# Block attention's own queries moved from ScalarE to GpSimd, with the counts and step masks re-ordered behind them

## The reference

```python
q, k = rope(x @ Wq.T), rope(x @ Wk.T)              # 16 heads of 16, 256 positions, 8 blocks of 32
km   = k.reshape(B, 8, 32, H, d).mean(axis=2)      # mean key of a block
gate = einsum('bshd,bnhd->bhsn', q, km)            # future blocks -1e30, own block +1e30
sel  = blocks among the 4 largest gates            # per query and head
scores = where(sel & causal, q @ k.T * d ** -0.5, -1e30)
o = softmax(scores) @ v                            # then normalised per head, times Wo
```

## Time and profile before

| | before |
|---|---|
| median of 3 runs | 682.59 us (682.48 to 682.76) |
| the profiled execution, its own time | 682.5 us |
| its span, first to last instruction | 680.3 us |
| TensorE busy | 655.0 us (96%) |
| VectorE busy | 493.7 us (73%) |
| ScalarE busy | 418.0 us (61%) |
| GpSimd busy | 298.1 us (44%) |
| mean granted TensorE clock | 0.999 |

### The profile page before, as it was taken

The page is one execution under the profiler, slowest core; times in us unless marked ns, Lnnn a source line. Parts: engine busy times, 40 slices in busy tenths (PEclk is TensorE's granted clock), DMA queues, the critical chain, the costliest instruction groups (busy, mean ns, idle before and its releaser), DMA issues.

```text
span 680.3 us, 13835 instructions
## 1 busy us (share of the span) xinstructions
PE 655.0 (96%) x4756; PEld 573.6 (84%) x4756; DVE 493.7 (73%) x1434; ACT 418.0 (61%) x1084; POOL 298.1 (44%) x301
## 2 busy tenths in 40 slices
PE   5999999999999999999999989999989999999997
PEld 3777888898888998888888865556889999999996
DVE  7897867877878687887797798897565544645444
ACT  3856158788888888798854689997553222222221
POOL 1584155556464655452344328997543500400000
PEclk9999999999999999999999999999999999999999
DMA  8902034444525344342740000303000000000000
GB/s 319 373 2 101 1 121 135 153 149 134 192 91 184 119 165 128 107 151 93 279 178 1 1 1 2 110 1 125 2 1 1 1 16 2 1 16 1 2 16 16
DMA packets 26725, 59.43 MB, mean 87 GB/s; under 512 B 3146, under 2 KB 12748, under 8 KB 26272
## 3 DMA queue, kind: packets, MB, share of 16 engines
q1 hardware_dynamic: 23584, 50.35, 21.7%
q0 software_dynamic: 3072, 8.20, 3.6%
HBM read 48.24 MB, written 10.49 MB: 86 GB/s over the span
## 4 chain that ended last, share of the span: by engine, by line
PE 75%; DVE 10%; ACT 7%; POOL 3%; issue 3%; DMA 0%; SPq 0%; ACTq 0%; POOLq 0%; DVEq 0%
PE bank L2284 11%; PE bank L2049 7%; PE bank L1983 6%; PE bank L2333 5%; PE bank L2040 5%; PE bank L2307 5%; PE bank L2145 4%; PE bank L2069 4%; PE bank L2060 4%; PE bank L1990 4%; ACT sb L1211 3%; PE bank L2111 3%; PE bank L2192 3%; PE bank L2347 2%; PE bank L1923 2%
## 5 line engine op out<-in xcount | busy, mean ns | idle before, releaser
L1072 ACT ACTIVATE sb<-bank,sb 128x256 f32<-128x256 f32 x128 | 59.5, 471 | 38.8 <-DVE sb L1573 37.8
L1279 ACT ACTIVATE h_parts<-sb 128x256 fp32r<-128x256 f32 x56 | 23.4, 418 | 72.6 <-DVE sb L1831 43.8
L2049 PE MATMUL bank<-sb 128*128 128x256 f32 x256 | 66.1, 381 | 0.0
L1822 DVE TENSOR_TENSOR sb<-sb,bank 128x256 f32<-128x256 f32 x56 | 23.4, 419 | 58.1 <-ACT sb L1235 58.1
L1573 DVE TENSOR_REDUCE sb<-bank 128x2 f32<-128x512 f32 x64 | 43.7, 683 | 27.1 <-PE bank L2049 26.6
L2284 PE MATMUL bank<-rounded,b_hi 128*128 128x256 f32 x224 | 63.1, 282 | 0.0
L2284 PE MATMUL bank<-rounded,b_lo 128*128 128x256 f32 x224 | 62.9, 281 | 0.0
L2284 PE MATMUL bank<-am_lo,b_hi 128*128 128x256 f32 x224 | 62.9, 281 | 0.0
L839 POOL DMA_INDIRECT expert_out<-sb x32 | 33.0, 1031 | 61.3 <-DVE sb L1515 47.4
L1235 ACT ACTIVATE sb<-bank 128x256 f32<-128x256 f32 x56 | 21.4, 382 | 61.6 <-PE bank L2284 61.6
L1079 ACT ACTIVATE sb<-sb 128x256 f32<-128x256 f32 x128 | 57.8, 505 | 0.1
(11 more groups left out here) (321 smaller groups left out, 1941.5 us busy)
## 6 DMA issues: line engine op xcount, KB each, us to landing
sb<-in_w_gate_up SPq DMA_DIRECT2D x32, 368.0 KB, 2.9
sb<-in_w_down SPq DMA_DIRECT2D x32, 256.0 KB, 2.7
sb<-in_w_pair SPq DMA_DIRECT2D x8, 704.0 KB, 4.0
expert_out<-sb SPq DMA_DIRECT2D x1, 4096.0 KB, 22.8
sb<-expert_out SPq DMA_DIRECT2D x8, 512.0 KB, 6.8
sb<-in_w SPq DMA_DIRECT2D x1, 1792.0 KB, 12.2
sb<-in_b SPq DMA_DIRECT2D x1, 1792.0 KB, 8.1
sb<-in_sw_up SPq DMA_DIRECT2D x1, 1536.0 KB, 9.0
```

The lines of the kernel that those rows point to most:

```text
L1072: act.activation(probs[:, u % 4, q, :], bank[3 + u % 2][:, q * S:(q + 1) * S], ACT.Exp, scale=-1.0, bias=row_min[:, u % 4, q:q + 1], accum ...
L2049: mm = pe.matmul(bank[3 + u % 2][:, q * S:(q + 1) * S], qb[i][:, h, b * S + q * P:b * S + (q + 1) * P], keys[:, h, b * S:(b + 1) * S], sta ...
```

## The change

Four edits, with what they need to be legal:

1. The own queries of groups 2 to 7 are no longer made by ScalarE inside the quads. GpSimd makes them before its counts, one `tensor_tensor` of 128x512 per group for both parities, into a new place `q_later`. That place is in `rounded`, where `x1T_hi` and `a13_hi` lie until the eighth low fill, so GpSimd waits for `fill_mm` 8; later the high parts of the masked activations go there, so those wait for the scores (`bl_s`).
2. GpSimd counts batch 1 alone and batches 2 and 3 together. The biases and the load of `b13` wait accordingly.
3. The product with the step mask and its split come behind the split of `b13`, the first activations and the first network weights.
4. `kmean` is written by two `tensor_tensor` instead of 16 `tensor_scalar`, and `own_bias(0)` comes behind the thirteenth fill copy instead of the sixteenth.

```diff
@@ block attention's buffers
-        q_par = r2.take(2, 2, S)
+        q_par = [r2.take(2, S) for _ in range(2)]
...
+            q_later = over("q_later", SB_COLS + 3 * TOK, 3 * TOK)
+        q_par += [Strip(q_later, at * TOK + G * 2 * S, 2 * S).take(2, S) for at in (1, 0, 2) for G in range(2)]
@@ count
-            ranks = rank.rearrange("p t (h n) -> p (t h) n", n=NB)[:, at:at + QT * H1, :]
+            ranks = rank.rearrange("p t (h n) -> p (t h) n", n=NB)[:, at:at + heads.stop - heads.start, :]
@@ sync
-            sp.wait_ge(rest_count, COUNTS * (B - 1))
+            sp.wait_ge(rest_count, COUNTS * 2)
             sp.dma_start(b13, t["b13"]).then_inc(ab_in, 16)
@@ gpsimd
+            pool.wait_ge(qkT_out, NT)
+            pool.wait_ge(bl_q, 4)
+            pool.wait_ge(fill_mm, 8)
+            for G in range(2, GROUPS):
+                b, k = G // 2, G % 2
+                pool.tensor_tensor(q_par[G], along(qkT[:, k, b * S:(b + 1) * S], (1, 2)), along(table("par_scale"), (2, S)),
+                                   ALU.mult).then_inc(bl_q, 2)
+
             pool.wait_ge(kmean_set, 5)
             pool.wait_ge(rest_beats, NB - 1)
-            for b in range(1, B):
-                count(pool, QT * H1 * b, slice(QT * H1 * (b - 1), QT * H1 * b), beats_rest, rest_beats, rest_count, COUNTS * (b - 1))
+            for n, (first, last) in enumerate(((1, 2), (2, B))):
+                count(pool, QT * H1 * first, slice(QT * H1 * (first - 1), QT * H1 * (last - 1)), beats_rest, rest_beats, rest_count,
+                      COUNTS * n)
...
-            pool.wait_ge(step_mask, 1)
-            for j in range(2):
-                pool.wait_ge(low_rank, j + 1)
-                pool.tensor_tensor(am_step[j], am_step[j], step_maskT, ALU.mult).then_inc(low_rank, 1)
-
             pool.wait_ge(ab_in, 32)
...
-            pool.wait_ge(low_rank, 4)
...
                 for k in kinds:
+                    if c < 2 and c + k:
+                        pool.wait_ge(bl_s, HG * {(0, 1): 4, (1, 0): 6, (1, 1): 8}[c, k])
...
-            low_rank_parts(0)
+            pool.wait_ge(low_rank, 2)
+            low_rank_parts(0, (0,))
             pool.wait_ge(w3_in, 32)
             for n, kind in enumerate(("x1", "w13")):
...
+            pool.wait_ge(step_mask, 1)
+            for j in range(2):
+                pool.tensor_tensor(am_step[j], am_step[j], step_maskT, ALU.mult).then_inc(low_rank, 1)
+            pool.wait_ge(low_rank, 4)
+            low_rank_parts(0, (1,))
             low_rank_parts(1, (0,))
@@ scalar
             def own_queries(G, par):
-                at_least(act, bl_s, HG * (G - 1))
-                act.activation(q_par[:, G % 2, par, :], qkT[:, k, b * S:(b + 1) * S], ACT.Copy,
+                act.activation(q_par[G][:, par, :], qkT[:, k, b * S:(b + 1) * S], ACT.Copy,
...
             def own_bias(G):
-                    act.wait_ge(rest_count, COUNTS * b)
+                    act.wait_ge(rest_count, COUNTS * min(b, 2))
...
+                if n == len(fills()) - 4:
+                    own_bias(0)
...
-            own_bias(0)
             own_bias(1)
             for Q in range(QUADS + 1):
...
-                if 1 < Q < QUADS and Q // 2 + 1 < GROUPS:
-                    own_queries(Q // 2 + 1, Q % 2)
@@ vector
-                for h in range(HG):
-                    at = (k * HG + h) * NB
-                    dve.tensor_scalar(kmean[:, k, :, at:at + NB], kblock[:, k, :].rearrange("p (b n) -> p b n", n=NB),
-                                      table("head_mean")[:, h:h + 1], None, ALU.mult).then_inc(kmean_done, 1)
+                own = slice(k * HG * NB, (k + 1) * HG * NB)
+                dve.tensor_tensor(kmean[:, k, :, own].rearrange("p b (h n) -> p b h n", n=NB),
+                                  along(kblock[:, k, :].rearrange("p (b n) -> p b n", n=NB), (2, HG)),
+                                  along(table("head_mean"), (1, B), (3, NB)), ALU.mult).then_inc(kmean_done, 1)
@@ tensor
-                    pe.wait_ge(kmean_done, 1 + KD * HG)
+                    pe.wait_ge(kmean_done, 1 + KD)
...
-                                  q_par[strip32, G % 2, par, q * P:(q + 1) * P],
+                                  q_par[G][strip32, par, q * P:(q + 1) * P],
```

## The result

The changed kernel takes **687.23 us** (median of 6 runs, 685.89 to 688.05), the kernel before 682.62 us in the same series (6 runs, 682.48 to 684.65): ratio 1.0062, 95% interval 1.0049 to 1.0076, so 4.6 us slower. The profiled execution, the slowest of the six, took 688.05 us with a span of 686.2 us and a mean granted clock of 0.995. One of the ten runs of a later experiment (e7) fell into a slow state, 929.96 us at a mean granted clock of 0.658, and is left out of its median.

A forecast was written before the change was run, and what follows sets the result against it. It took ScalarE's copy, transpose, copy loop to bound the quads and a VectorE counting chain the stretch before them. -1.0 + 5.9 + 0.7 = +5.6 us on 682.5 gave 688.1 us, range 683.0 to 690.8.

The forecast's parts named there:

- What bounds it: Block attention: ScalarE's loop of copy, transpose, copy sets the quads' period; ahead of them a chain through VectorE's counting.
- Own queries off ScalarE: In the quads: twelve instructions of 0.50 us go, but they only filled a wait for TensorE's transpose; 0 us.
- Mean keys: Ahead of the first quad: two instructions for 16 start the counting earlier and L1773 avoids GpSimd's copies; -1.0 us.
- own_bias(0) earlier: On ScalarE: waits for VectorE's counts, with three fill copies and own_bias(1) queued behind it; costs nothing undisturbed.
- Six collisions: Before the first minimum: six VectorE counting steps each meet one GpSimd multiplication and lose 0.98 us; +5.9 us.
- Fall of the clock: TensorE idles 5.7 us before the share turns, so its clock falls; +0.7 us, bounds 0 and 1.6.
- Counts and masks: GpSimd's counts start later but end by 431, before the first bias needing batch 2; cost 0.
- Its signs of being right: Seventh to twelfth counting steps near 1.3 us, first minimum near 405.9, quads still 4.62 and 4.32 apart, clock under 1.00.
- VectorE keeps the port: Rival, 10%: VectorE's gaps of 0.03 us are too short for GpSimd, so the counts lose nothing; 681.5 us.
- the own queries bound the quads: Rival, 4%: removing ScalarE's own queries takes 12 x 0.5 us off the quads, besides the -1.0; 675.5 us.
- the clock keeps up: Rival within the forecast's 76%: the collisions occur but TensorE's clock does not fall; 687.4 us.
- The second rival: 10%: only one or two collisions, as comparisons without waits between them hold off the other multiplications; 682.5 to 683.5 us.

The follow-up runs named there:

- e7: Changed kernel with GpSimd's six multiplications held until VectorE's last counting step, so they meet only the comparisons; 684.89 us, ratio 1.0025.
- e1: Changed kernel with the own queries of groups 2 to 7 made by ScalarE in the quads again; 682.64 us, ratio 0.9986.
- e2: Changed kernel with GpSimd making two own queries after VectorE's last comparisons and four after the count of batch 1; 682.62 us, ratio 0.9985.
- e10: The kernel of e2 with own_bias(0) behind the sixteenth fill copy again; 682.68 us, ratio 0.9991.
- e11: The kernel before with only the two-instruction mean keys added; 682.40 us, ratio 0.9987.
- e6: Changed kernel with TensorE turning the first shares eight more times while it would stand idle; 687.45 us, ratio 1.0054.
- e8: The kernel before with only the own queries of groups 2 to 7 moved to GpSimd; 688.56 us, ratio 1.0076.
- e5: Changed kernel with each of GpSimd's six multiplications made twice, in two rounds; 691.73 us, ratio 1.0123.
- e3: Changed kernel with GpSimd writing zeros by memset instead of multiplying, so those own queries are left out; 682.37 us, ratio 0.9982.

## Why the prediction was right

The forecast was 688.1 us in a range of 683.0 to 690.8; the median is 687.23. The mechanism is the one forecast; how near the sum comes is in part luck. By its own steps:

- **What bounds it** held. Own queries off ScalarE: put at 0, measured 0.00 (e1 against e2).
- **Mean keys**, put at -1.0: the counting starts 1.10 us earlier after the reduction. L1773's share was put at 0.6 and is 1.81 - 1.23 = 0.58.
- **own_bias(0) earlier** "costs nothing undisturbed". That is so, but it misses a gain: undisturbed it is what lets 0.45 us of the mean keys' gain through (e10, e11). With the collisions in place the first minimum follows VectorE directly, so it gives nothing in the changed kernel.
- **Six collisions** of 0.98 us, +5.9: there are six, in a row from the seventh step on, and they lie on the chain. The term is too large by 1.5 us, in the price of one collision. A multiplication of this form takes GpSimd 1.02 us (e2, undisturbed), not the 1.29 of the earlier trace rows, which is an addition whose operands repeat nothing; and the loss measured is 0.74. The prediction had taken 0.98 and 1.05 from collisions with other GpSimd instructions.
- **Fall of the clock**, +0.7: it fell where it was expected, and cost 1.22 (e6), within the bounds of 0 and 1.6. What failed is the use of the start of the span as its measure: of what runs slowly behind the share turns it counted eight products, 0.7 us, while here the low level lasted over the transposes of line 2264 and the scores, 1.67 instead of 0.94 for the latter alone. It also put the share turns off the chain, and they delay the first transposes by 0.20 us; without them in the slow stretch the price was 0.75 (e8). And in the rows of the start the profile lists the granted clock at 1.00, so that the clock is what slows them was assumed there, not read. The eight share turns at a granted 0.50 take the same 1.94 us as the eight products at 7.00 in the earlier trace rows, which speaks for it.
- **Counts and masks**, 0: GpSimd's masks start at 427.07, before the 431 allowed; batches 2 and 3 together take 427.07 - 416.58 = 10.5 us instead of 14.2, and the rest of the span did not grow (210.5 against 210.6).
- **Sum**: -1.10 + 4.43 + 1.23 = 4.56 against -1.0 + 5.9 + 0.7 = 5.6. Two errors of opposite sign, -1.5 and +0.5, make the total look better than its terms.
- **Its signs of being right.** The seventh to twelfth steps are the long ones, but take 0.94 to 1.10 us, not near 1.3. The first minimum at 405.74 beside the forecast 405.9, and the profiled 688.05 us beside 688.1, are luck: the profiled execution reached block attention 1.44 us later than the one before did, which about makes up for the collision term. TensorE idled 4.33 us, not 5.7, since, measured from the reduction, the counts were done some 1.5 us sooner than forecast.

Of the rivals, that VectorE keeps the port is ruled out by the six long steps, that the own queries bound the quads by e1, and that the clock keeps up by the slices. The second rival's outcome did not occur, and its ground was false as well: e5 and e7 show GpSimd getting in between comparisons that have no waits between them. The prediction had read the earlier trace rows, where one GpSimd multiplication stood for 5.46 us, as a VectorE stream without gaps holding the port. What held that one is open; no run here tried it. A stream of that kind kept GpSimd waiting for 4 us there, and took turns with it here, even in e7 where the first comparison was already running.

The Trainium skill's rule, cited in the prediction (SBUF — State Buffer, Who interferes with whom), says that the engine that issues first blocks the other until it is done. The sign follows from it. Read as a whole GpSimd instruction lost per step, as in the prediction, it gives an estimate of 6 x 1.02 = 6.1 us; measured are 4.4, and the measurement decides. A step and GpSimd's multiplication together take 1.03 us, not 1.02 + 0.26, so a step's own length is spent within GpSimd's time and hardly on top of it. The longer comparisons of e7 are nearer to the rule: each loses 0.84 us, and GpSimd loses time too, 1.55 instead of 1.02 for the multiplication shown.

## What to carry to other kernels

An idle engine is not a free place if what it runs reads SBUF while the busy engine's critical instructions have two operands there: look at what runs beside it before moving work, and count collisions one by one. Here the same six instructions cost 4.4 us beside a serial chain of short two-operand steps and nothing when they start 7 to 17 us later. And a removed cost that was covered (the own queries' 6 us of busy time on ScalarE) is worth nothing: look at what takes its place in the gap.

## What the runs showed of the hardware

- A VectorE instruction of two SBUF operands and a GpSimd multiplication of 128x512 took turns one for one in the changed kernel, e5, e7 and e8, whether or not VectorE's stream had gaps: 0.74 us lost per counting step, 0.81 per comparison in e5. The earlier trace rows is a case in layer 0 where they did not. A GpSimd memset of the same size costs VectorE nothing (e3), and a VectorE minimum with only one operand in SBUF loses nothing beside a multiplication (0.28 us in e7).
- GpSimd's multiplication, whose queries and scale are both repeated, took 1.02 us, an addition of the same size that repeats nothing 1.29; no run says why.
- The granted clock does not fall at the same wait each time. TensorE waits 2.09 us for VectorE at the same instruction near 503 us in the kernel before and in e1; before keeps its clock and e1 loses it. TensorE's timeline and the slice that shows the level, for the kernel before and then for e1:

```profile
503.08 0.47 PE L2307 MATMUL bank<-x_hi,w_hi_rest 128*128 128x256 f32 x2 [2.09 <-DVE sb L1822]
```

```profile
504.00:506.00 2.00, 2.00 (x19) 1.96 (x17) 1.56 (x2) 0.92 (x3) 1.31 (x1) 1.00 0.00 0
```

```profile
502.56 0.48 PE L2312 MATMUL bank<-x_hi,w_hi_rest 128*128 128x256 f32 x2 [2.09 <-DVE sb L1827]
```

```profile
504.00:506.00 2.00, 2.00 (x11) 2.00 (x11) 1.38 (x2) 0.40 (x2) 1.83 (x2) 0.50 0.00 0
```

  Such a fall is the 1.1 us in the last column of the stage table: the eight traces with 211.7 have it between 502 and 517 us, the four with 210.5 or 210.6 do not. The first column varies too: eight products of the start of the span take 3.88 us in the kernel before and 4.87 in the profiled execution of the changed one, where nothing was edited; the granted clock is listed at 1.00 there in both, so no trace shows the reason:

```profile
8.74 4.87 PE L1934 MATMUL bank<-sb 128*128 128x417 f32 x8
```

  In e7 the clock was down to 0.64 and 0.50 in the slices from 404 and 406, after a wait of only 1.73 us. So this kernel has 1 to 2 us of scatter outside the stages that an edit touches, and stage lengths out of the traces are the finer measure.
- That scatter is not blind to the kernel. Of the 32 runs of e1, e2 and e3, 28 have a mean granted clock of 0.997, the value of their profiled executions with the fall near 503 us; of the 27 of the kernel before in the same series, 8 have. This takes back part of the 1.1 us that their middle stages gain, and fits the medians lying only 0.6 to 0.9 us below. It does not follow the edit alone either: of e10, which is e2 with one edit more and ran on another chip, 2 of 11 runs have that value. What decides it is open.
